# Turning one half of a scan's result by 32x32 blocks and DMAs instead of on TensorE, in a one-core language-model layer

## What is computed

```
h = table[ids]                                  # rows of 256 floats, NaN -> 0
x = layernorm(h)
f, i, c = sigmoid(x @ Wf.T), sigmoid(x @ Wi.T), g(x @ Wh.T)
s[t] = f[t] * s[t-1] + i[t] * c[t], s[-1] = 0.5 # a scan along each sequence
h = h + s                                       # the residual sum
y = layernorm(h)
r = relu(ternary(w_fc) y * scale + gate * low_rank(y))
out = h + ternary(w_proj) (r * r) * scale       # hidden width 1024
```

## Time and profile before

| what | us |
|---|---|
| median of 3 runs | 964.75 (964.73 to 965.76) |
| the profiled execution | 964.22 |
| its span, first to last instruction | 962.2 |
| PE busy | 906.2 (94%) |
| DVE busy | 722.7 (75%) |
| ACT busy | 787.4 (82%) |
| POOL busy | 422.8 (44%) |
| hardware DMA queue, share of 16 engines' span | 22.7% |

### The profile page before, as it was taken

The page is one execution under the profiler, slowest core; times in us unless marked ns, Lnnn a source line. Parts: engine busy times, 40 slices in busy tenths (PEclk is TensorE's granted clock), DMA queues, the critical chain, the costliest instruction groups (busy, mean ns, idle before and its releaser), DMA issues.

```text
span 962.2 us, 17305 instructions
## 1 busy us (share of the span) xinstructions
PE 906.2 (94%) x5313; PEld 525.9 (55%) x5313; DVE 722.7 (75%) x1250; ACT 787.4 (82%) x1159; POOL 422.8 (44%) x459
## 2 busy tenths in 40 slices
PE   1577999999999999999999999999999999999986
PEld 1233656655566566555656665566566555655654
DVE  6677687877777878787777878777878787777663
ACT  4447788998888889888888998888889888888775
POOL 6542455544445554444455544445554444433110
PEclk8788999999999999999999999999999999999999
DMA  4211232122222212222222121223212222222210
GB/s 138 55 26 26 72 71 54 43 63 56 71 71 71 69 38 58 58 60 71 71 71 60 35 68 49 71 71 71 71 45 50 61 58 70 71 67 55 34 53 35
DMA packets 161754, 57.91 MB, mean 60 GB/s; under 512 B 140358, under 2 KB 160400, under 8 KB 161728
## 3 DMA queue, kind: packets, MB, share of 16 engines
q1 hardware_dynamic: 155584, 53.38, 22.7%
q0 software_dynamic: 6144, 4.21, 1.9%
HBM read 19.81 MB, written 16.78 MB: 38 GB/s over the span
## 4 chain that ended last, share of the span: by engine, by line
PE 88%; ACT 4%; DVE 3%; DMA 2%; issue 1%; SPq 1%; POOL 0%; ACTq 0%; DVEq 0%
PE bank L652 33%; PE y_ps L626 22%; PE bank L696 21%; PE bank L700 5%; PE turned L709 3%; PE bank L610 3%; ACT normed L391 1%; DMA x_cols<-x_rows 1%; DMA sq<-w_fc 1%; ACT relu L438 1%; ACT x_rows L398 1%; SPq L257 0%; ACT sq L451 0%; ACT sq L371 0%; DVE hid L983 0%
## 5 line engine op out<-in xcount | busy, mean ns | idle before, releaser
L696 PE MATMUL bank<-x_cols,fc_t 128*128 128x512 f16 x1024 | 263.7, 380 | 0.7 <-issue 0.7
L652 PE MATMUL bank<-x_cols,w_hi 128*128 128x512 f16 x768 | 231.1, 383 | 22.2 <-DMA x_cols<-x_rows 19.4
L321 POOL TENSOR_SCALAR var_eps<-moments 128x4 f32<-128x4 f32 x64 | 60.5, 945 | 420.8 <-DVE moments L784 420.8
L652 PE MATMUL bank<-x_cols,w_lo 128*128 128x512 f16 x768 | 231.1, 383 | 0.0
L626 PE MATMUL y_ps<-proj_t,sq_hi 128*128 128x256 bf16 x1024 | 225.5, 273 | 2.7 <-DVE sq_lo L931 2.5
L626 PE MATMUL y_ps<-proj_t,sq_lo 128*128 128x256 bf16 x1024 | 225.5, 273 | 0.0
L438 ACT ACTIVATE relu<-bank,relu_scale 128x512 f32<-128x512 f32 x256 | 165.7, 690 | 13.7 <-PE bank L700 13.7
L311 POOL DMA_INDIRECT rows_raw<-table,idx_now x128 | 148.4, 1159 | 59.5 <-issue 31.0
L696 PEld LDWEIGHTS bank<-x_cols,fc_t 128*128 128x128 bf16 x1024 | 100.2, 98 | 114.2 <-issue 1.5
L931 DVE TENSOR_TENSOR sq_lo<-sq,sq_hi 128x1024 f16<-128x1024 f32 x128 | 150.5, 1215 | 12.1 <-ACT sq L451 12.0
L391 ACT ACTIVATE normed<-h,shift,rstd 128x256 f32<-128x256 f32 x256 | 132.7, 597 | 17.3 <-POOL shift L329 16.7
(11 more groups left out here) (131 smaller groups left out, 942.2 us busy)
## 6 DMA issues: line engine op xcount, KB each, us to landing
out<-out_sb SPq DMA_DIRECT2D x32, 512.0 KB, 3.2
rows_raw<-table,idx_now POOLq DMA_INDIRECT x128, 2.6
x_cols<-x_rows SPq DMA_TRANSPOSE x128, 2.7
sq<-w_fc SPq DMA_DIRECT2D x1, 1024.0 KB, 7.2
pj_raw<-w_proj SPq DMA_DIRECT2D x1, 1024.0 KB, 9.4
w_raw<-wf SPq DMA_DIRECT2D x1, 256.0 KB, 2.7
w_raw<-wi SPq DMA_DIRECT2D x1, 256.0 KB, 2.9
w_raw<-wh SPq DMA_DIRECT2D x1, 256.0 KB, 3.9
```

What stands on the lines that cost most here:

```text
L652: ins = pe.matmul(bank[gate_bank[p]][:, :], w[:, k, q, :], x_part(0, par, part)[:, :, k, :], start=(k == 0 and w is w_hi and part == 0), s ...
L696: pe.matmul(dst[:, :], fc_t[:, k, f * P:(f + 1) * P], x_part(1, 0, part)[:, :, k, :], start=(k == 0 and part == 0), stop=False)
```

## The change

The turn of half e = 0 leaves TensorE. VectorE transposes hid's half 0 in blocks of 32x32 into a new tile `hid_blocks` (128 x 512 f32) right behind the scan of that half (`turn_blocks`). SP then issues sixteen plain DMAs (`move_blocks`), one for each place (q, i) in the 4 x 4 grid of blocks: each copies 32 partitions x 4 tiles x 32 floats (runs of 128 bytes, 16 KB in all) from partitions 32i of `hid_blocks` to partitions 32q of `hid_rows`, in which the half then stands in rows. TensorE keeps the four transposes of half 1. The residual sum becomes two operations: the channels 0 to 127 from `hid_rows` in SBUF, and the channels 128 to 255 from `turned` in PSUM; `measure` waits for both. In SP's step the sixteen DMAs stand between the two pairs of transposing DMAs, and the store of the output moves behind the second pair. To make room, a tile used only while the weights are prepared (`pj_a`) now lies on `out_sb`.

```diff
+        hid_blocks = sb("hid_blocks", [P, CHUNK])
+        hid_rows = sb("hid_rows", [P, TILES, P])
...
-        pj_a = sb("pj_a", [P, KD, HID])
+        pj_a = out_sb[:, :, :, :].rearrange("p a j d -> p a (j d)")
...
+            def move_blocks(c, par):
+
+                sp.wait_ge(blocks_ready, c + 1)
+                wait(sp, h1_low, c)
+                for i in range(B):
+                    from_blocks = hid_blocks[BLOCK * i:BLOCK * (i + 1), :].rearrange(
+                        "r (j q c) -> r j q c", j=TILES, q=B)
+                    for q in range(B):
+                        sp.dma_start(hid_rows[BLOCK * q:BLOCK * (q + 1), :, BLOCK * i:BLOCK * (i + 1)],
+                                     from_blocks[:, :, q, :]).then_inc(blocks_moved[par], 16)
...
                     turn_rows(1, n - 1, 0)
-                if not isinstance(n, int) or n > 1:
-                    store(n - 2, par)
+                if known_below(n, N):
+                    move_blocks(n, par)
                 if known_below(n, N - 1):
                     wait(sp, gate_done, 6 * n)
                     pass_on(sp, sp_passed, n)
                     turn_rows(0, n + 1, 1 - par)
+                if not isinstance(n, int) or n > 1:
+                    store(n - 2, par)
...
                         for j in range(TILES):
-                            for e in range(KD):
-                                ins = pe.transpose(turned_rows[:, j, e * P:(e + 1) * P],
-                                                   hid[:, e, j * P:(j + 1) * P], ident[:, :])
+                            ins = pe.transpose(turned_rows[:, j, P:D], hid[:, 1, j * P:(j + 1) * P], ident[:, :])
                         ins.then_inc(hid_turned, 1)
...
+                def turn_blocks():
+
+                    dve.wait_ge(scanned, 4 * n + 2)
+                    wait(dve, blocks_moved[1 - par], 16 * B * B * (h + par))
+                    dve.transpose(hid_blocks[:, :], hid[:, 0, :]).then_inc(blocks_ready, 1)
...
                 if front:
                     scan(0)
+                    turn_blocks()
...
                 if front:
+                    dve.wait_ge(blocks_moved[par], 16 * B * B * (h + 1))
+                    dve.tensor_tensor(h1[:, par, :, 0:P], hid_rows[:, :, :], h0[:, par, :, 0:P], ALU.add)\
+                        .then_inc(h1_low, 1)
                     dve.wait_ge(hid_turned, n + 1)
-                    dve.tensor_tensor(h1[:, par, :, :], turned_rows, h0[:, par, :, :], ALU.add).then_inc(h1_ready, 1)
+                    dve.tensor_tensor(h1[:, par, :, P:D], turned_rows[:, :, P:D], h0[:, par, :, P:D], ALU.add)\
+                        .then_inc(h1_ready, 1)
+                    dve.wait_ge(h1_low, n + 1)
                     dve.wait_ge(h1_ready, n + 1)
                     measure(1, n, h1[:, par, :, :])
```

More of the change, by code:

```diff
@@ L44 @@
 RELU_TOP = 2.0 ** 6
+BLOCK = 32
+B = P // BLOCK
 FIRST_LOOP, LAST_LOOP = 5, N - 4
@@ L195, in build @@
         hid_turned = sem("hid_turned")
+        blocks_ready = sem("blocks_ready")
+        blocks_moved = [sem("blocks_moved_even"), sem("blocks_moved_odd")]
+        h1_low = sem("h1_low")
         h1_ready = sem("h1_ready")
@@ L979, in scan @@
                     dve.wait_ge(value_ready, 2 * n + e + 1)
-                    wait(dve, hid_turned, n)
+                    if e == 0:
+                        wait(dve, blocks_ready, n)
+                    else:
+                        wait(dve, hid_turned, n)
                     for s in range(CHUNK // T):
```

## The result

The changed kernel takes 1077.99 us (4 runs, 1074.42 to 1082.51) against 965.25 of the kernel before in the same comparison: a ratio of 1.116, 95% interval 1.1131 to 1.119. The forecast was 956 with a range from 951 to 985. It is slower by 11.6%, and the profiled execution took 1074.42 us, 110.2 more than the one of before. The interval is 0.3% to either side, so the 0.2% that was named as the limit of what runs can tell was somewhat too fine.

The account below looks back on a forecast made before the run. TensorE (PE), busy 94% of the span, was taken as the bound. 964.2 - 12.5 for the transposes + 3.7 at the start = 955.4; with 0.5 from profiled run to median, 956 us, range 951 to 985 for 8 in 10.

Parts of the forecast that it names:

- one costs 0.37 + 0.05 = 0.42 to 0.47 us; 0.50 is the far end: Issue of one block DMA on SP, sixteen a step: 0.43 us taken, 0.50 if issues queue.
- a slack of 0.2 and 0.4: Spare time forecast per step: 0.2 us in the residual sum's loop, 0.4 before PE needs the next chunk's columns.
- The sign that the prediction named: In the trace: block issues 0.46 us or more apart, or landing 2.3 or more, means PE idles every step.
- The gain on PE: TensorE, each step: four of eight transposes go, 0.43 us less, 27.72 to 27.29; 12.5 us over 29 steps.
- The landing: Block DMA from its issue to landed data: 1.9 us taken, with 1.6 and 2.7 as ends.
- The columns' deadline: Transposing DMAs behind the sixteen land at 508.34, PE's gates start at 508.96; spare 0.4 us, gone at 0.46 an issue.
- Rival B: The loop through the residual sum becomes the bound, DVE waiting for the last block; 970 or 992 us; chance 0.38.
- the closed loop through the sum: Early scan, block DMAs, residual sum, norm, candidate, next early scan: period 27.1 us, just under PE's 27.29.
- d: How far the last block lands beyond 506.0 us; some 28 steps each grow by it, time 956 + 28 d.
- Rival C: The same loop or the columns' deadline takes back about PE's gain, 0.24 to 0.38 us: 963 to 967; chance 0.12.
- The start: Steps 0 and 1, the path hidden by nothing: 3.0 us and 0.7 later, +3.7 in all, bounds 0 and 5.
- Rivals D and E: D: something else waits instead, 958 to 962 us, chance 0.02. E: sixteen DMAs don't overlap, over 1600, chance 0.01.

Follow-up runs that it names:

- tests 1 and 8: Kernel before, with seven and then eight series of small DMAs on SP after its last store, for issue times: 0.59 to 0.64 us SBUF to SBUF.
- test 6: Changed kernel with the half turned through HBM, one DMA writing and four reading back instead of sixteen block DMAs: 954.84 us, ratio 0.9889.
- test 5: Changed kernel with 28 more transposes of the identity on PE ahead of its wait for columns, from the third step on: 1059.37 us, ratio 1.0972.

## Why the prediction was wrong

- **The step that failed** is the term "one costs 0.37 + 0.05 = 0.42 to 0.47 us; 0.50 is the far end": measured 0.60 + 0.045 = 0.645. The nearest rows were nearest in size only. They had HBM on one side (the two at the start in one run, the store in four runs of 1 KB in each partition), and the new DMAs have SBUF on both; tests 1 and 8 show that to be the difference (HBM's side in several runs of 128 bytes cost 0.60 to 0.63, as much as SBUF on both, in three forms of four). Sixteen times 0.21 is 3.4 us, against a slack of 0.2 and 0.4. The far end was set close to rows of the same kind, so it was no bound. Even among the issues at the program's start the trace of before has longer ones than the two that were read; they are loads from HBM with more than one run in each partition (the three of the first one's form took 0.41, 0.46 and 0.47):

```profile
2.17 0.47 SPq L244 DMA_DIRECT2D w_raw<-wh  x1
4.60 0.58 SPq L249 DMA_DIRECT2D sq<-w_fc  x1
```

- **The sign that the prediction named**, issues 0.46 or more apart and then idle time of PE in every step, came just so.
- **What held.** The gain on PE: 27.28 us a step in test 6 and 27.29 forecast. The landing 1.8 (1.9), the block transpose 0.71 (0.69), hidden behind `emit` as said, the first issue 0.87 us behind the scan's end (1.03). The columns' deadline: with 0.645 in the forecast's own formula the columns land at 497.47 + 16 x 0.645 + 1.29 + 2.7 = 511.8, a step of about 30.3, and 30.5 was measured. What the forecast did not say is that this deadline is a loop: it counted from a scan at a fixed time, and the chain above shows that the scan itself waits for PE's projection.
- **Rival B** had the direction and the term that decides, but named the closed loop through the sum. In the changed kernel that loop is 0.4 to 0.6 us shorter than the columns' loop, as DVE's waits of 0.38 and 0.63 us for PE show. Its price for d stopped at 1.3 us; the step grew by 3.25 against the 27.29.
- **Rival C** named the columns' deadline beside the loop, but for a loss of 0.38 us a step at most.
- **The clock was left out.** A wait of 3 us on PE is not worth 3 us: it cost 18.6 us beside the loop's own 81.8 (test 5). The prediction has no term for it.
- **The start**: +3.7 expected, 7.2 measured at step 2. The same issue time accounts for the difference (sixteen of 0.645 are 3.4 longer). In test 6 it was 94.59 - 91.94 = 2.7.
- **Rivals D and E** did not happen. The DMAs overlap: each lands 1.8 us after its issue, and they are issued 0.645 apart. What is serial is SP's issuing.

## What to carry to other kernels

Count the DMAs that an edit issues and multiply by the issue time of that very kind of DMA (which memories on the two sides), before looking at bytes, packets or landing; copies within SBUF (0.59 to 0.64 us), and three forms of four with HBM's side in several runs of 128 bytes (0.60 to 0.63), were dearer here than those with HBM's side in one run (0.42 to 0.43). Ask what stands behind them in the issuing queue: there the next step's input paid, not the data moved. Where a turn within SBUF is made of many DMAs, as the sixteen here, a way through HBM with one write and a few reads can be shorter, although it lands twice: 954.84 us here against 1077.99. Whether another engine could have issued a part of the sixteen was not tried.

## What the runs showed of the hardware

- The issue of a DMA on SP took, as the medians of the series of tests 1 and 8, 0.59 to 0.64 us from SBUF to SBUF in the six forms tried (one of them also alone, 0.586), 0.42 to 0.43 with HBM on one side in one run, and with HBM's side in several runs of 128 bytes 0.60 to 0.63 in three forms and 0.43 in the fourth. The 256 KB of test 6 from SBUF to HBM took 0.34, the store (512 KB, four runs of 1 KB in each partition) 0.37 before, 0.41 in the changed kernel and 0.42 in test 6. The eight loads of up to 256 KB at the start of the kernel before took 0.40 to 0.47. Between two of the sixteen issues lie 0.045 us.
- A 16 KB copy within SBUF in runs of 128 bytes, from 32 to 32 partitions, landed 1.8 us after its issue began (median of 512 in the changed kernel, 2.8 the longest); 64 KB in 128 partitions 2.1 (test 1).
- A block transpose of 128x512 f32 on VectorE took 0.71 us (all 32 of the changed kernel).
- With waits of 3 us in each step TensorE's mean granted clock was 0.90 to 0.95 over nine of 29 steps (0.50 from 878.30 to 882.30 us in one of them) and 1.00 over the other twenty; what makes the difference between these steps was not tried. With 28 transposes of the identity in that time it was 1.00 from 192 to 930 us.
